# Graph attention whose row term becomes the bias of ScalarE's copies, with a later division, in a four-block transformer on one core

## Chip, core and metric

One core of one Trainium2 chip runs the whole computation in one launch. The metric is the device time in microseconds (us); three runs of the kernel before gave 1117.23, 1118.01 and 1122.63, so its median is 1118.01. Engines are named as the profile does: PE (TensorE matmuls), PEld (TensorE weight loads), DVE (VectorE), ACT (ScalarE), POOL (GpSimd), SP (SyncE, which issues DMAs). Each engine runs its own instructions strictly in order and waits on semaphores.

## What is computed

The input is `x` (4 graphs of 256 rows of 256) and a context (4 x 256 x 64). Four blocks follow one another: a two-layer graph attention, a mixture of 8 experts (top 2), a learned mix with a sparse similarity, and a transformer layer with 32 heads and 32 experts (top 8). The change touches only the first block:

```python
x = x + gat(ctx, adj=_layernorm(x))           # two layers of:
feat = einsum('nf,hfo->hno', x, W)            # 8 heads of 32
attn_self  = einsum('hno,ho->hn', feat, a_self)
attn_neigh = einsum('hno,ho->hn', feat, a_neigh)
e = attn_self[:, :, None] + attn_neigh[:, None, :]     # 256 x 256 a head
e = leaky_relu(e, 0.2) + MASK_VAL * (1.0 - adj)
alpha = softmax(e, axis=-1)
out = elu(einsum('hnm,hmo->hno', alpha, feat) + b)
```

Everything is in float32; the edge term and some projections go through PE as `float32r`, a rounded form of it.

## The kernel before, in words

**Rounds, units, quads.** The graph attention handles (layer, graph) pairs in `ROUNDS` = 8 rounds, layer 0 for the four graphs and then layer 1. A round has `UNITS` = 8 units, one for each head; a unit is a 256 x 256 matrix of edges, held as two tiles of 128 rows side by side (128 x 512). Four units form a quad. The 64 units run through a software pipeline that every engine writes out as a loop over slots k; in slot k an engine treats unit k less its own lag, in the order of the code. `starts_in(k, lead)` names the round that starts `lead` slots later, `quad_at(k, lag)` the quad due `lag` slots after its base, `round_at(k, lag)` the same for a round of layer 1. The loop ends at `LAST` = 75.

**The stations of unit k.** (1) PE `edges` writes the logits into one of two PSUM banks `ZB` (L606): the neighbour term, the same for all rows, by a matmul whose stationary operand is -1 in the row of head h and whose moving operand is `st_parts`, 256 columns read twice; then the row term by two matmuls of 256 columns with `st_parts` as stationary operand and a constant as moving operand. (2) ACT `copy_z` (L1025) copies the bank into `alpha`, a ring of six, in one 128 x 512 copy, times 0.2 in odd units. (3) The leaky part: DVE `leak` in even units, two POOL instructions in odd ones. (4) DVE `edges` adds the mask and takes the row minimum. (5) ACT `exps` takes the exponential of each tile with the row sum. (6) PE `turn` transposes four 128 x 128 blocks into `PTB`. (7) ACT or DVE copies them to `alphaT` (`copy_T`; DVE in odd units, but for every sixteenth).

**The stations of quad j.** DVE `invert` takes reciprocals of the row sums in slot 4j+7. PE `weigh` in slot 4j+9 multiplies by the features into `OB`, and spreads the reciprocals by 16 small matmuls. DVE `divide` (slot 4j+10) multiplies the two; POOL `positive` and ACT `exp_out` (also 4j+10) form the two halves of the elu, DVE `elu` (4j+11) joins them into `h1T`, the input of layer 1, or `x1T`, which PE turns (`turn_x1`, 17 slots after the round's start), DVE adds to `xs` (`add_x1`, 18) and measures (19), and POOL takes the inverse deviation of (20).

**Before a round.** Four slots before it starts, PE `prep` computes the self and neighbour terms of all heads into `MISC`, and DVE `prep` splits them into a high and a low part, `st_parts`. PE `features` computes one tile of features three slots ahead and the other two slots ahead, and ACT `copy_features` takes them out one slot ahead; its start is where I cut the rounds below. In layer 0 `prep` and `features` contract over 64 values in one matmul, in layer 1 over 256 in two.

**What sets the order.** Nothing but the slots and these waits: PE's `edges(k)` needs `copy_z(k-2)` finished, since there are two `ZB` banks; `turn(k)` needs `exps(k)`; `weigh(j)` needs `divide(j-2)`. SP loads all expert weights (24 loads of 512 KB) during the first 48 us, behind the small loads, one of which is the indicator array `ind_f` of 48 x 8 x 144 values, which ACT rounds to float32r once (L1072).

## Time and profile before

| What | Value |
|---|---|
| median of three runs | 1118.01 us |
| the profiled execution itself | 1124.08 us, with a span of 1122.3 us from its first to its last instruction |
| mean granted TensorE clock | 0.947 of 2.4 GHz |
| PE / PEld / DVE / ACT / POOL busy over the span | 93% / 75% / 76% / 54% / 38% |
| graph attention, first feature copy to last edge copy | 12.4 to 182.8 us |
| DVE's transposed copies (L1590, 128 x 512) | 28, mean 685 ns |
| ACT's edge copies (L1029, 128 x 512) | 64, mean 593 ns |
| ACT's exponentials (L1042, 128 x 256) | 128, mean 505 ns, with a sum read of 196 ns each |
| POOL's two instructions of an odd unit (L1386, L1389) | 32 each, mean 2035 and 1314 ns |
| DVE's 128 x 256 copy out of PSUM (L1601) | 16, mean 422 ns |

A matmul's busy time overlaps that of its neighbours, and so does an activation's, so what one of them costs on a full engine is the distance from its start to the next start. A profile execution is one sample; this one lies 0.5% above the median of the runs. The clock column of a table of stretches gives the granted share of the full 2.4 GHz: 0.50 is 1.2 GHz. Before 55 us it has no record and prints 1.00.

### The profile page before, as it was taken

The numbers are of one execution on the slowest core, as the hardware profiler recorded it, in microseconds if no ns is written. First come the engines' busy times: TensorE is split into PE (matmuls) and PEld (weight loads), VectorE is DVE, ScalarE is ACT, GpSimd is POOL, SyncE is SP. The second block draws the span as 40 slices with busy tenths as digits, with TensorE's granted clock in tenths as the row PEclk, the third lists the DMA queues.
The fourth block names the chain that finished last, engine by engine and source line by source line (L and its number), as shares of the span: only waits on it lengthen the run. The fifth ranks groups of instructions, "written<-read, shape, count | busy, mean of one in ns | idle before, by whom it ended". The sixth has DMA issues, their size and how long they took to land.

```text
span 1122.3 us, 20301 instructions
## 1 busy us (share of the span) xinstructions
PE 1041.2 (93%) x6046; PEld 845.9 (75%) x6046; DVE 857.1 (76%) x2625; ACT 605.4 (54%) x1686; POOL 422.8 (38%) x365
## 2 busy tenths in 40 slices
PE   5888988899999369999999999999998999999997
PEld 3555665456666247899999999999987888888886
DVE  6878687567773689877777777776878878878877
ACT  3578686533333167777777778777953222222221
POOL 5679696251110543332423334222323323323221
PEclk9979697599999589999999999999999999999999
DMA  9600000311111420110001010000010111111111
GB/s 298 242 1 1 1 2 20 104 38 48 45 43 32 125 67 6 44 37 3 17 32 39 2 34 2 1 2 1 16 30 15 44 55 42 50 48 42 53 45 37
DMA packets 50259, 49.46 MB, mean 44 GB/s; under 512 B 4976, under 2 KB 43440, under 8 KB 50176
## 3 DMA queue, kind: packets, MB, share of 16 engines
q1 hardware_dynamic: 47024, 41.96, 11.8%
q0 software_dynamic: 1872, 5.11, 1.7%
q10 hardware_dynamic: 1280, 1.38, 0.5%
q8 instruction: 41, 0.67, 0.2%
q14 instruction: 42, 0.34, 0.1%
HBM read 43.32 MB, written 5.11 MB: 43 GB/s over the span
## 4 chain that ended last, share of the span: by engine, by line
PE 76%; DVE 10%; ACT 6%; POOL 4%; issue 3%; DMA 1%; SPq 0%; ACTq 0%; DVEq 0%; POOLq 0%
PE bank L58 13%; PE bank L59 12%; PE bank L60 12%; PE bank L936 6%; PE bank L957 4%; PE bank L831 4%; PE bank L839 4%; PE bank L858 4%; PE bank L946 3%; PE bank L958 2%; PE bank L629 2%; PE bank L645 2%; PE bank L615 1%; POOL rest L1386 1%; ACT alpha L1042 1%
## 5 line engine op out<-in xcount | busy, mean ns | idle before, releaser
L1451 POOL TENSOR_TENSOR rot_s<-swap,rq 128x512 f32<-128x512 f32 x64 | 88.6, 1385 | 194.4 <-ACT swap L1233 194.3
L1109 ACT ACTIVATE silu<-bank 128x512 f32<-128x512 f32 x66 | 39.6, 600 | 173.4 <-PE bank L60 173.4
L1246 ACT ACTIVATE prob<-prob,pmin 128x128 f32<-128x128 f32 (+1 forms) x256 | 113.8, 449 | 5.5 <-DVE pmin L1992 5.5
L2011 DVE TENSOR_TENSOR o_ring<-bank,o_ring 128x256 fp32r<-128x256 f32 x128 | 54.3, 424 | 80.1 <-ACT o_ring L1262 78.6
L936 PE MATMUL bank<-kv,norm 128*128 128x128 f32 (+1 forms) x512 | 106.1, 330 | 6.4 <-DVE norm L1985 6.0
L1834 DVE SCALAR_TENSOR_TENSOR xs<-bank,wt,xs 128x256 f32<-128x256 f32 x264 | 109.1, 477 | 0.1
L1407 POOL TENSOR_TENSOR gate_r<-gate_w,gate_r 128x256 fp32r<-128x256 f32 x31 | 36.5, 1176 | 177.2 <-ACT gate_r L1102 177.2
L1262 ACT ACTIVATE o_ring<-bank 128x256 fp32r<-128x256 f32 x128 | 48.5, 379 | 75.8 <-PE bank L958 75.7
L58 PE MATMUL bank<-wo_r,o_ring 128*128 128x256 f32 x256 | 82.4, 322 | 0.0
L2004 DVE TENSOR_SCALAR prob<-prob,pinv 128x128 f32<-128x128 f32 (+1 forms) x256 | 77.1, 344 | 4.6
L1992 DVE CUSTOM_DVE_ANT_0 prob<-bank,causal 128x128 f32<-128x128 f32 (+1 forms) x256 | 80.4, 352 | 0.1
L957 PE MATMUL bank<-probT,kv 128*128 128x256 f32 x256 | 76.9, 382 | 3.3 <-DVE o_ring L2011 3.3
L1812 DVE TENSOR_TENSOR hidf<-silu,bank 128x512 f32<-128x512 f32 x66 | 45.4, 688 | 44.8 <-ACT silu L1109 43.2
L58 PE MATMUL bank<-actT_r,wqk_r 128*128 128x512 f32 x144 | 71.8, 499 | 2.5 <-DVE kv L1958 2.5
L936 PEld LDWEIGHTS bank<-kv,norm 128*128 128x128 f32 x512 | 67.6, 192 | 7.4 <-DVE norm L1985 6.7
L58 PE MATMUL bank<-down_r,hidT 128*128 128x256 f32 x248 | 70.2, 283 | 2.7 <-DVE xs L1834 1.4
L60 PE MATMUL bank<-wo_r,o_ring 128*128 128x256 f32 x256 | 72.2, 282 | 0.0
L59 PE MATMUL bank<-wo_r,o_ring 128*128 128x256 f32 x256 | 72.0, 281 | 0.0
L1386 POOL TENSOR_SCALAR rest<-alpha 128x512 f32<-128x512 f32 x32 | 65.1, 2035 | 13.6 <-ACT alpha L1029 11.1
L60 PE MATMUL bank<-down_r,hidT 128*128 128x256 f32 x248 | 70.2, 283 | 0.0
L59 PE MATMUL bank<-down_r,hidT 128*128 128x256 f32 x248 | 70.1, 283 | 0.0
L1256 ACT ACTIVATE probT<-bank 128x384 f32<-128x384 f32 x128 | 62.9, 492 | 13.4 <-PE bank L946 7.9
(297 smaller groups left out, 3126.4 us busy)
## 6 DMA issues: line engine op xcount, KB each, us to landing
gate_w<-in_Wg SPq DMA_DIRECT2D x33, 128.0 KB, 2.2
up_w<-in_Wu SPq DMA_DIRECT2D x33, 128.0 KB, 2.2
down_w<-in_Wd SPq DMA_DIRECT2D x33, 128.0 KB, 2.2
w_all<-in_w_gate SPq DMA_DIRECT2D x8, 512.0 KB, 10.7
w_all<-in_w_up SPq DMA_DIRECT2D x8, 512.0 KB, 10.3
w_all<-in_w_down SPq DMA_DIRECT2D x8, 512.0 KB, 10.6
wq_g<-in_Wq SPq DMA_DIRECT2D x4, 1024.0 KB, 5.5
wo_g<-in_Wo SPq DMA_DIRECT2D x4, 1024.0 KB, 5.3
```

The costliest lines, as they stand in the source:

```text
L58: pe.matmul(out, lhs[0], rhs[0], start=first, stop=False)
L59: pe.matmul(out, lhs[0], rhs[1], start=False, stop=False)
L60: return pe.matmul(out, lhs[1], rhs[0], start=False, stop=last)
L936: mm = pe.matmul(S_BANK[u % 2][:, nt * P:nt * P + (nt + 1) * P], qT[:, (u // 2) % 4, b2 * N + nt * P:b2 * N + nt * P + P], kT[:, b * N:b * ...
L957: pe.matmul(O_BANK[:, 0:N], vt[:, t, :], probT[:, u % 2, 0:N], start=True, stop=False)
L1246: ins = act.activation(prob[:, u % 4, nt * P:nt * P + (nt + 1) * P], prob[:, u % 4, nt * P:nt * P + (nt + 1) * P], ACT.Exp, bias=pmin[:, u ...
L1256: act.activation(probT[:, u % 2, :], PT_BANK[:, 0:3 * P], ACT.Copy).then_inc(S["pT_copied"], 1)
L1386: pool.tensor_scalar(rest[:], alpha[:, k % RING, :], 1.0 / NEG - 1.0, 0.0, ALU.mult, ALU.min).then_inc(S["z_rest"], 1)
L1451: pool.tensor_tensor(rot_s[:, m % 2].rearrange("p (b n) -> p b n", b=2), swap[:, m % 2].rearrange("p (b n) -> p b n", b=2), bcast(tab[:, 1 ...
L1834: ins = dve.scalar_tensor_tensor(xs[:, t, :], DB[2 * (mod % 2) + j // 2][:, j % 2 * D:j % 2 * D + D], w, xs[:, t, :], ALU.mult, ALU.add)
L1992: ins = dve.tensor_tensor_reduce(out=prob[:, u % 4, nt * P:nt * P + (nt + 1) * P], in0=S_BANK[u % 2][:, nt * P:nt * P + (nt + 1) * P], in1 ...
L2004: ins = dve.tensor_scalar(prob[:, u % 4, nt * P:nt * P + (nt + 1) * P], prob[:, u % 4, nt * P:nt * P + (nt + 1) * P], pinv[:, u % 4, nt:nt ...
```

## The change

The row term leaves the 128 x 512 edge matrix. The indicator array shrinks to two values a head (`ind[:, h, 0]` for the neighbour term, `ind[:, :, 1]` for all heads' row terms). A new PE step `self_columns(r)`, three slots before a round, computes the row term of all eight heads as columns (two matmuls of 8 columns) into `MISC`; a new DVE step `keep_columns(r)` in the same slot copies them into `s_col`, times 0.2 for odd heads. `edges(k)` on PE is a single matmul of 256 columns, and `copy_z(k)` on ACT makes two copies of 128 x 256 from it, one a tile, each with its column of `s_col` as bias.

Besides that: ACT hands every sixteenth unit's transposed copy to DVE; `divide` moves one slot later, `positive`, `exp_out` and `elu` two; the steps behind a round of layer 1 (`turn_x1`, `add_x1`, the measure and the inverse) move two slots later, and with them the ends of the three normalisations and `LAST`; DVE's `neighbours(0)` moves ahead of `measure(1)`. A spare array keeps the other arrays nearly where they were. The whole diff:

```diff
--- before.py
+++ after.py
@@ -31,7 +31,6 @@
 QUAD = 4
-PAD = 16
 RING = 6
...
@@ -179,7 +178,7 @@
         qkT = first_use.enter_context(nc.sbuf_tensor("qkT", [FC, 2, B * N], F32))
-        ind_f = first_use.enter_context(nc.sbuf_tensor("ind_f", [TR, GH, P + PAD], F32))
+        ind_f = first_use.enter_context(nc.sbuf_tensor("ind_f", [TR, GH, 2], F32))
         first_use.close()
...
@@ -188,10 +187,13 @@
         wst1 = sb_early("wst1", [P, HC, TR])
-        ind = sb_early("ind", [TR, GH, P + PAD], F32R)
+        ind = sb_early("ind", [TR, GH, 2], F32R)
         st_parts = sb_early("st_parts", [TR, 2, N], F32R)
...
         neg_rstd = sb_early("neg_rstd", [P, T])
+        sb_early("spare", [P, 1120])
+        s_col = sb_early("s_col", [P, 2, NT, GH])
+        s_scale = sb_early("s_scale", [P, NT, GH // 2, 2])
         row_sum = sb_early("row_sum", [P, 2, NT, QUAD])
...
@@ -313,7 +315,7 @@
-            "st_ready", "feat_ready", "feat_copied", "st_copied", "adj_ready",
+            "st_ready", "col_ready", "col_copied", "feat_ready", "feat_copied", "st_copied", "adj_ready",
             "adj_bias", "z_ready", "z_copied", "z_rest", "z_pool", "z_dve", "edge_done", "alpha_done", "alphaT_ready",
...
@@ -342,8 +344,8 @@
         ALLQ = ROUNDS * QUADS
-        LAST = ALL + 11
-        NORM_AT, TURN_AT, ROUTE_AT = (ALL, ALL + 2, ALL + 8), (ALL + 2, ALL + 4, ALL + 9), (ALL + 4, ALL + 6, ALL + 10)
+        LAST = ALL + 13
+        NORM_AT, TURN_AT, ROUTE_AT = (ALL, ALL + 2, ALL + 10), (ALL + 2, ALL + 4, ALL + 11), (ALL + 4, ALL + 6, ALL + 12)
...
@@ -366,7 +368,7 @@
         def copied_by_dve(k):
-            return k % 2 == 1 and k % 16 != 15
+            return k % 2 == 1
...
@@ -591,6 +593,18 @@
+                def self_columns(r):
+
+                    if r == 0:
+                        pe.wait_ge(S["ind_done"], 1)
+                    else:
+                        pe.wait_ge(S["col_copied"], r)
+                    pe.wait_ge(S["st_copied"], 2 * r + 2)
+                    for nt in range(NT):
+                        mm = pe.matmul(MISC[:, N + nt * GH:N + nt * GH + GH], st_parts[:, r % 2, nt * P:nt * P + P],
+                                       ind[:, :, 1], start=True, stop=True)
+                    mm.then_inc(S["col_ready"], 1)
+
                 def features(r, nt):
...
@@ -606,19 +620,11 @@
                     r, h = divmod(k, UNITS)
-                    if k == 0:
-                        pe.wait_ge(S["ind_done"], 1)
-                    if h == 0:
-                        pe.wait_ge(S["st_copied"], 2 * r + 2)
                     if k >= 2:
                         pe.wait_ge(S["z_copied"], k - 1)
-                    pe.matmul(ZB[k % 2].rearrange("p (u n) -> p u n", u=NT), ind[:, h, 0:P],
-                              bcast(st_parts[:, r % 2, :], 1, NT), start=True, stop=False)
-                    for nt in range(NT):
-                        mm = pe.matmul(ZB[k % 2][:, nt * N:nt * N + N].rearrange("p (u n) -> p u n", n=PAD),
-                                       st_parts[:, r % 2, nt * P:nt * P + P],
-                                       bcast(ind[:, h, P:], 1, N // PAD), start=False, stop=nt == NT - 1)
-                    mm.then_inc(S["z_ready"], 1)
+                    pe.matmul(ZB[k % 2][:, 0:N], ind[:, h, 0:1].to_broadcast([TR, P]), st_parts[:, r % 2, :],
+                              start=True, stop=True
+                              ).then_inc(S["z_ready"], 1)
...
@@ -692,6 +698,7 @@
                     features(0, nt)
+                self_columns(0)
                 for k in range(-1, LAST):
...
@@ -699,12 +706,14 @@
                         edges(k + 1)
+                    if (r := starts_in(k, 3)) is not None:
+                        self_columns(r)
                     for nt in range(NT):
...
                         weigh(j)
-                    if (r := round_at(k, 17)) is not None:
+                    if (r := round_at(k, 19)) is not None:
                         turn_x1(r)
...
@@ -1026,7 +1035,13 @@
                         act.wait_ge(S["alphaT_ready"], k - RING + 1)
-                    act.activation(alpha[:, k % RING, :], ZB[k % 2][:], ACT.Copy, scale=NEG if k % 2 else 1.0).then_inc(S["z_copied"], 1)
+                    r, h = divmod(k, UNITS)
+                    if h == 0:
+                        act.wait_ge(S["col_copied"], r + 1)
+                    for nt in range(NT):
+                        ins = act.activation(alpha[:, k % RING, nt * N:nt * N + N], ZB[k % 2][:, 0:N], ACT.Identity,
+                                             bias=s_col[:, r % 2, nt, h:h + 1], scale=NEG if k % 2 else 1.0)
+                    ins.then_inc(S["z_copied"], 1)
...
@@ -1078,7 +1093,7 @@
                         copy_T(k - 5)
-                    if (j := quad_at(k, 1)) is not None:
+                    if (j := quad_at(k, 3)) is not None:
                         exp_out(j)
...
@@ -1377,7 +1392,7 @@
             for k in range(LAST):
-                if (j := quad_at(k, 1)) is not None:
+                if (j := quad_at(k, 3)) is not None:
                     positive(j)
...
@@ -1392,7 +1407,7 @@
                     inverse(k // 2)
-                if (r := round_at(k, 20)) is not None:
+                if (r := round_at(k, 22)) is not None:
                     inverse(r)
...
@@ -1507,6 +1522,8 @@
+                dve.memset(s_scale[:, :, :, 1:2], NEG)
+                dve.memset(s_scale[:, :, :, 0:1], 1.0)
                 chain.link(dve.memset(wst0[:], 0.0))
...
@@ -1565,6 +1582,14 @@
+                def keep_columns(r):
+
+                    dve.wait_ge(S["col_ready"], r + 1)
+                    if r >= 2:
+                        dve.wait_ge(S["z_copied"], UNITS * (r - 1))
+                    dve.tensor_tensor(s_col[:, r % 2].rearrange("p u h -> p (u h)"), MISC[:, N:N + NT * GH],
+                                      s_scale[:].rearrange("p u a j -> p (u a j)"), ALU.mult).then_inc(S["col_copied"], 1)
+
                 def leak(k):
...
@@ -1628,8 +1653,9 @@
                 prep(0)
+                keep_columns(0)
+                neighbours(0)
                 measure(1)
-                neighbours(0)
                 for k in range(LAST):
...
@@ -1647,15 +1673,17 @@
                         prep(r)
+                    if (r := starts_in(k, 3)) is not None:
+                        keep_columns(r)
                     if (j := quad_at(k, -2)) is not None:
                         invert(j)
-                    if (j := quad_at(k, 1)) is not None:
+                    if (j := quad_at(k, 2)) is not None:
                         divide(j)
-                    if (j := quad_at(k, 2)) is not None:
+                    if (j := quad_at(k, 4)) is not None:
                         elu(j)
-                    if (r := round_at(k, 18)) is not None:
+                    if (r := round_at(k, 20)) is not None:
                         add_x1(r)
-                    if (r := round_at(k, 19)) is not None:
+                    if (r := round_at(k, 21)) is not None:
                         measure(r)
...
@@ -2101,10 +2129,10 @@
-    ind = np.zeros((TR, GH, P + PAD), np.float32)
+    ind = np.zeros((TR, GH, 2), np.float32)
     for h in range(GH):
-        ind[[h, ROW + h], h, :P] = -1.0
-        ind[[GH + h, ROW + GH + h], h, P:] = -1.0
+        ind[[h, ROW + h], h, 0] = -1.0
+        ind[[GH + h, ROW + GH + h], h, 1] = -1.0
...
```

## Rows read from the trace of the kernel before

**Rows 1.** Stretches, one a round: length; PE, PEld, DVE, ACT, POOL busy; clock; DMA share, GB/s.

```profile
...
12.36:32.96 20.60, 14.69 (x45) 9.97 (x45) 18.41 (x52) 11.15 (x32) 17.47 (x16) 1.00 1.06 369
32.96:58.61 25.65, 24.99 (x132) 15.57 (x130) 20.73 (x61) 15.94 (x48) 15.43 (x11) 1.00 0.56 194
58.61:81.25 22.64, 20.47 (x126) 12.96 (x126) 18.08 (x56) 15.99 (x50) 17.50 (x12) 0.70 0.00 1
81.25:99.00 17.75, 16.09 (x132) 10.83 (x132) 15.48 (x48) 15.29 (x49) 15.96 (x11) 1.00 0.01 2
99.00:117.33 18.33, 16.00 (x132) 10.82 (x132) 15.67 (x50) 15.66 (x50) 16.43 (x11) 1.00 0.00 1
117.33:143.09 25.76, 25.03 (x133) 15.78 (x132) 16.42 (x52) 15.81 (x49) 16.60 (x11) 0.60 0.00 1
143.09:161.94 18.85, 16.68 (x138) 11.27 (x136) 17.31 (x54) 15.81 (x49) 16.99 (x13) 1.00 0.00 1
161.94:182.18 20.24, 18.45 (x118) 12.14 (x119) 14.89 (x52) 13.76 (x42) 15.75 (x12) 0.66 0.01 2
...
```

**Rows 2.** Timeline of PE in round 5: start us, busy us, instructions.

```profile
...
127.14 0.79 PE L615 MATMUL bank<-st_parts,ind 48*128 48x512 f32 x1
127.74 0.63 PE L618 MATMUL bank<-ind,st_parts 48*128 48x256 f32 x2
128.29 1.94 PE L590 MATMUL bank<-actT,wst 128*48 128x256 f32 x4
...
134.56 2.07 PE L602 MATMUL bank<-w,actT 128*128 128x256 f32 x4
136.56 1.94 PE L645 MATMUL bank<-alphaT,rq 128*32 128x256 f32 x16
...
139.28 1.12 PE L629 MATMUL bank<-ident,alpha 128*128 128x128 f32 x4
140.32 0.52 PE L615 MATMUL bank<-st_parts,ind 48*128 48x512 f32 x1
...
```

**Rows 3.** Timeline of PE in round 1.

```profile
...
46.27 1.08 PE L590 MATMUL bank<-ctx_all,wst 64*48 64x256 f32 x2
47.28 1.11 PE L629 MATMUL bank<-ident,alpha 128*128 128x128 f32 x4
...
```

**Rows 4.** Timeline of PE in round 3.

```profile
...
86.63 0.50 PE L615 MATMUL bank<-st_parts,ind 48*128 48x512 f32 x1
86.97 0.40 PE L618 MATMUL bank<-ind,st_parts 48*128 48x256 f32 x2
87.30 0.66 PE L629 MATMUL bank<-ident,alpha 128*128 128x128 f32 x4
...
```

**Rows 5.** Timeline of ACT in round 3.

```profile
...
85.13 0.61 ACT L1029 ACTIVATE alpha<-bank 128x512 f32<-128x512 f32 x1
85.61 0.53 ACT L1042 ACTIVATE alpha<-alpha,edge_min 128x256 f32<-128x256 f32 x1
...
86.10 0.53 ACT L1042 ACTIVATE alpha<-alpha,edge_min 128x256 f32<-128x256 f32 x1
...
87.47 0.51 ACT L1060 ACTIVATE g_exp<-g_out,bT 128x256 f32<-128x256 f32 x1 [0.75 <-DVE g_out L1602]
87.89 0.58 ACT L1029 ACTIVATE alpha<-bank 128x512 f32<-128x512 f32 x1
...
```

**Rows 6.** Timeline of ACT: four copies of 128 columns out of PSUM.

```profile
...
381.17 1.15 ACT L1195 ACTIVATE actT<-bank,lnw 128x128 f32<-128x128 f32 x4 [1.04 <-PE bank L896]
...
```

**Rows 7.** Groups by line and form, 0 to 330 us: busy us, mean ns, idle before.

```profile
...
L1314 ACT ACTIVATE sim<-bank 128x256 f32<-128x256 f32 x8 | 3.0, 380 | 0.4 <-PE bank L557 0.3
...
```

**Rows 8.** Waits from 12 to 190 us: who for whom, total, times, longest.

```profile
...
ACT g_exp L1060 <- DVE g_out L1602: 29.6, 15, 4.1
...
POOL g_pos L1364 <- DVE g_out L1602: 22.4, 15, 3.9
DVE g_pos L1601 <- PE bank L650: 15.2, 8, 5.2
...
```

## The prediction

> **What bounds the kernel now.** The edit lives in the graph attention, eight rounds of eight units (a unit is one head of one graph). I read the stretch table first, cut where ScalarE starts the copy of each round's features [rows 1]. The reader is to see two kinds of round. Rounds 3, 4 and 6 (17.75, 18.33, 18.85 us) have the TensorE clock at its full level, 2.4 GHz, and no engine full: PE 16.0 to 16.7, POOL 16.0 to 17.0, DVE 15.5 to 17.3, ACT 15.3 to 15.8 busy. Rounds 1 and 5 (25.65, 25.76) have PE busy for 25.0 of it and everybody else below 21: there PE is the bound, because it runs at 1.2 GHz. Round 5 shows it as a mean clock of 0.60. Round 1 is printed as 1.00, but its four transposes take 1.11 us [rows 3], the same as at 139.28 in round 5 while the clock is down (1.12) [rows 2], so it was slow too. Rounds 2 and 7 are mixed. Round 0 (20.60) has PE idle for 6 us and DVE busy for 18.4: no PE edit moves it.
>
> Next the PE order of a slow round, start to start [rows 2]: transposes of a unit 139.28 to 140.32, 1.04; its edge term, one 512-column and two 256-column matmuls, 127.14 to 128.29, so 1.15; `prep` 1.9; `features` 2.0 a tile; `weigh` 136.56 to 139.28, so 2.7. In layer 0 `prep` takes 46.27 to 47.28, 1.0 [rows 3]; a tile of `features` has the same contraction and the same 256 columns there, and I give it 1.0 too. A layer-0 round at 1.2 GHz is 8 x (1.04 + 1.15) + 2 x 2.7 + 1.0 + 2.0 = 25.9 us; round 1 has 25.65, so the sum is the explanation of that round. With layer-1 `prep` and `features` it is 28.8; round 5 is shorter because its first 2.6 us and its last part are fast. Last the table of waits [rows 8]: in-order engines lose 29.6 us (ACT) and 22.4 (POOL) on `g_out`, that is on `divide`, which itself waits 15.2 for PE's `weigh`.
>
> **The change, part by part.**
> Edge matmuls: 64 units go from three matmuls (1024 columns) to one of 256. The new one costs a half of the pair of 256-column ones: 0.28 of 1.15 at 1.2 GHz [rows 2]; at 2.4 GHz 0.17 of 0.67 [rows 4]. Saved: 0.87 or 0.50 us of PE a unit, 7.0 or 4.0 a round. On the path only where PE is the bound. `self_columns` adds two matmuls of 8 columns a round; no row has the form, between 0.05 and 0.56 (the price of the 256-column pair); I take 0.2. A slow PE round is then 25.9 - 7.0 + 0.2 = 19.1 in layer 0, 28.8 - 6.8 = 22.0 with layer-1 `features`.
>
> ScalarE's copies: one immediate-scale copy of 512 columns, 0.48 start to start [rows 5], becomes two of 256 with a bias column. The two ends: the exponential of `exp_out`, same size, bias column, from SBUF, 0.42 start to start [rows 5]; and the four 128-column copies out of PSUM with a scale column in 1.15 us [rows 6]: 0.37 of it for the last, so 0.26 each. 256 more columns cost a copy out of PSUM about 0.60 - 0.38 = 0.22 us (512 columns in [rows 5] against 256 in [rows 7]), 128 more 0.11, so 0.37. A pair is 0.74 to 0.84, and a unit grows by 0.26 to 0.36; I take 0.30, nearer the PSUM row. A round: ACT slots now 8 x (0.48 + 2 x 0.49) + 4.5 x 0.48 (transposed copies, the same form) + 2 x 0.42 + 0.48 = 15.2; plus 2.4, less half a transposed copy (0.24) = 17.3. So ACT takes POOL's place as the busiest, and its 2 to 3 us of spare time per fast round is spent. This is the price of the edit.
>
> The Trainium skill ("ScalarE: Activation LUTs", What ACT_TABLE_LOAD costs) gives an ACTIVATE 186 ns + 0.833 ns an element and adds 93 ns for each column operand, with 93 ns of overlap back to back. By it, an estimate, the pair costs 2 x 0.40 against 0.52, +0.28 a unit, inside my ends; the trace's fixed part of a 512-column copy agrees (0.60 us busy, 0.48 apart).
>
> DVE: 4 transposed copies come over from ACT (0.69 us each, one in two rounds), `keep_columns` adds a 128x16 product a round (below the 0.42 us of 128x256 rows, above nothing: 0.15). About 0.5 us a round on an engine with over 2 us spare in fast rounds. Its place matters more. It sits in the slot of `features`, and waits for `self_columns`, which on PE stands behind that slot's transposes and edge matmul; `elu` and the next edges queue behind it, and ACT's exponentials for them. And PE waits in `self_columns` for DVE's `prep` one slot after it was issued, where before it waited three slots later; `features` and `weigh` queue behind. From 0 to about 1 us a round (half a slot of 2.2); seven rounds; I take 1.5 in all, 0 and 7 as ends.
>
> The later `divide`, `positive`, `exp_out`, `elu`: no work is added. The waits of [rows 8] have one or two slots more of cover; a wait that is not the bound gives nothing by itself, but ACT, now fullest, needs those 2.5 us a round. I count this as what lets rounds be near ACT's sum, not as a term. `turn_x1`, `add_x1` and `measure` go with it; the next user of those banks is `features` of round 7, one slot behind `add_x1` of round 4, so it still fits. The two further slots at the end contain no instruction of their own. Tail: 0 (-0.5 to +1).
>
> Start: the indicator load shrinks from 221 KB to 3 KB and ACT's copy of it with it, but PE was waiting for the weights then; `neighbours(0)` moves ahead of a `measure`; `self_columns` and `keep_columns` stand ahead of the first copy. Together -0.1 (-1 to +0.5), in round 0.
>
> **The sum.** A fast round today is some 1.2 us above its fullest engine (18.3 against 16.0 to 17.0 in rounds 3, 4, 6 [rows 1]). Above ACT's 17.3 that gives 18.5. A slow one cannot be under 19.1 or 22.0. The clock: PE now has 65% or so of its fast work left, so I expect it at 1.2 GHz for most of the stage, with full speed after the dense stretches (`features` and `weigh` stand together, and in round 5 the clock rises right behind them: the 512-column matmul at 140.32 takes 0.52 where the one at 127.14 took 0.79 [rows 2]). If a fifth of the time is fast, PE's 22.0 becomes 22.0 / 1.2 = 18.3, no longer above ACT. I take 19.0 to 19.4 in layer 0 and 19.5 with layer-1 features. New minus old by round: 0: -0.1; 1: 19.4 - 25.65 = -6.3; 2: 19.0 - 22.64 = -3.6; 3: 19.5 - 17.75 = +1.8; 4: +1.2; 5: -6.3; 6: +0.6; 7 (no features): 18.8 - 20.24 = -1.4. Sum -14.1; with the new waits +1.5: **-12.6**. The profiled execution took 1124.08 (span 1122.3), so 1111.5 for such a one; the median of the runs is 6 us under it, and 1118.0 - 12.6 = **1105.5**.
>
> What follows the stage starts earlier and is not shortened. Where the clock changes after it may shift by some us either way: 2 us in the range.
>
> **Rivals.**
> A, ACT alone is the bound: the clock or PE's shorter queue keeps PE out of it, and the later division removes all of ACT's waits. Seven rounds of 17.8: 20.5 + 124.6 = 145.1 against 169.8 now (rounds 0 to 7), -24.7: 1093. For: 29.6 us of ACT's waits. Against: fast rounds today never reach their fullest engine.
>
> B, the low clock eats the gain: today's three fast rounds (54.9 us) become slow ones of 21 to 22 while rounds 1, 2, 5 get to 20 to 21. (20.5 + 2 x 20 + 4 x 21.5 + 20) = 166.5: -3.3, 1115. For: rounds 3, 4, 6 keep the full clock with PE 88% busy, and the stage has dropped to 1.2 GHz in rounds 2, 5 and 7 with lighter stretches. The Trainium skill ("TensorE: Matmul & The Clock Gate", Part 1) states the same direction, activity releases the throttle, and its Part 4 that transposes do not count as busy the same way. By that rule the edge matmuls removed are what kept the clock up, and B or C would be the outcome; the trace agrees that a PE full of transposes and edge terms stays at 1.2 GHz from 127.1 to 136.6 us [rows 2].
>
> C, slower: at 1.2 GHz the heavy slots stop overlapping. `prep` 3.2, `features` + `weigh` 6.2, `features` 3.3, `weigh` 4.1 are PE's, and in the other four slots PE must wait for ACT (17.3 / 8 = 2.16 each), since only two edge banks let it run ahead: 16.8 + 8.6 = 25.4 for rounds 3 to 6, 22.5 for 1 and 2, 21 for 7: 20.5 + 45 + 101.6 + 21 = 188.1, +18.3: 1136 in full, 1126 if half of it comes. It is slower from a mean of 21.3 us over rounds 1 to 7. Against: PE ran 25.0 of 25.7 us in round 1, so slots do overlap.
>
> **Chances.** Forecast 0.55; A 0.20; B 0.15; C 0.10. Range 1096 to 1116: all of the forecast's own spread (ACT's ends give 2 us either way on seven rounds, waits -1.5 to +5.5, the clock's share 5), half of A, and B. The least that a measurement tells from no change is 0.5%, 5.6 us. Faster by more: forecast, A and a part of B, 0.79; within 0.5%: most of B, 0.12; slower: 0.09.
>
> **What would show it.** Edge matmul 0.28 apart at 1.2 GHz and PE busy under 20 us a round; two ACT copies 0.37 to 0.42 apart and ACT busy 17 to 18 a round; rounds 1, 2 and 5 near 19.5 and rounds 3, 4, 6 about 1 us longer than now; a mean clock under 0.75 over the stage; the wait of `g_exp` below 10 us in total; ACT as the largest name in the chain between 30 and 180 us. It is wrong if rounds 3, 4 and 6 grow past 21.3, if a new wait on the column product is above 1 us a round, or if a transfer or table load shows up in the stage.

## The result, and the profile after

The changed kernel takes 1115.06 us (median of 14 runs, 1114.27 to 1118.13); the kernel before, on the same chips, 1121.32 (14 runs, 1117.23 to 1126.49). The ratio is 0.9949, 95% interval 0.9933 to 0.9964: faster by 5.7 us, less than half of the 12.6 that were forecast. The median lies just inside the forecast's range of 1096 to 1116, and near rival B's 1115. A part of the distance from 1105.5 to 1115.06, 3.3 us, is the base: the three first runs gave 1118.01, the larger sample 1121.32. The profiled execution took 1115.82 (span 1114.0), 8.3 us under that of before, which lay 2.8 above its median. So the rounds below explain 8 us, of which the medians hold 6.

Stretches of the changed kernel, one a round as in [rows 1], last the stretch from the last pair of edge copies to just past the end of the stage:

```profile
...
11.79:31.02 19.23, 11.60 (x33) 6.67 (x33) 18.15 (x55) 13.00 (x39) 16.50 (x15) 1.00 1.04 364
31.02:53.76 22.74, 18.52 (x115) 10.72 (x113) 19.97 (x64) 16.98 (x56) 15.22 (x11) 0.85 0.71 247
53.76:74.38 20.62, 17.70 (x112) 10.40 (x112) 17.28 (x57) 17.05 (x56) 16.30 (x12) 0.67 0.00 2
74.38:92.92 18.54, 16.10 (x118) 10.11 (x118) 14.04 (x45) 17.06 (x56) 15.55 (x11) 0.82 0.01 1
92.92:112.86 19.94, 15.83 (x118) 9.97 (x118) 16.22 (x53) 17.18 (x57) 15.85 (x11) 0.83 0.01 2
112.86:132.87 20.01, 16.05 (x118) 10.09 (x118) 16.24 (x52) 17.16 (x56) 15.84 (x11) 0.83 0.00 1
132.87:152.97 20.10, 16.83 (x122) 10.60 (x122) 17.99 (x57) 17.24 (x56) 16.23 (x13) 0.83 0.01 2
152.97:173.00 20.03, 15.45 (x104) 9.17 (x104) 17.26 (x50) 15.08 (x49) 16.24 (x12) 0.67 0.00 1
173.00:194.50 21.50, 16.66 (x132) 12.50 (x132) 15.50 (x50) 9.97 (x28) 8.63 (x10) 0.66 0.19 58
...
```

The stage is 8.45 us shorter: its first feature copy comes 0.57 earlier, rounds 0 to 7 take 161.21 against 169.82, and the tail 20.9 against 20.2. From ScalarE's last copy of the stage (193.94, before 202.39) to the end both have 920 us. The reader is to see that rounds 4 to 7 now all take 19.9 to 20.1, and that no engine is full in any of them: ACT has 17.2 (15.1 in round 7), PE 15.5 to 16.8, DVE 16.2 to 18.0. PE's clock stands at 0.82 or 0.83 in rounds 3 to 6, where it was 1.00 in three of them. With two levels, 0.50 and 1.00, a mean of 0.82 is full speed for about two thirds of a round.

Who waited for whom in the changed kernel, 12 to 190 us (total, times, longest), against [rows 8]:

```profile
...
POOL rest L1401 <- ACT alpha L1042: 27.8, 14, 3.8
...
ACT alpha L1042 <- PE bank L625: 24.2, 18, 2.5
...
DVE alpha L1604 <- POOL alpha L1404: 19.4, 19, 1.9
PE bank L635 <- DVE alphaT L1615: 13.6, 7, 3.0
...
POOL g_pos L1379 <- DVE g_out L1627: 3.5, 2, 2.8
...
ACT g_exp L1075 <- DVE g_out L1627: 1.7, 1, 1.7
...
```

The waits for `g_out` are gone (29.6 to 1.7 for ACT; 22.4 to 3.5 for POOL). Others have taken their place: POOL for ACT's copies 27.8 us (11.1 before), ACT for the edge matmul 24.2 (12.4), DVE for POOL 19.4 (11.8), PE for DVE's transposed copies 13.6 (3.4). One round shows how they hang together. PE in round 5:

```profile
...
116.21 1.09 PE L635 MATMUL bank<-ident,alpha 128*128 128x128 f32 x4 [2.17 <-DVE alphaT L1615]
117.23 0.58 PE L625 MATMUL bank<-st_parts,ind 48*128 48x256 f32 x1
117.73 1.93 PE L651 MATMUL bank<-alphaT,rq 128*32 128x256 f32 x16
119.44 1.08 PE L656 MATMUL bank<-ident,row_sum 128*32 128x128 f32 x16
120.45 1.12 PE L635 MATMUL bank<-ident,alpha 128*128 128x128 f32 x4
121.50 0.58 PE L625 MATMUL bank<-st_parts,ind 48*128 48x256 f32 x1
...
122.72 0.38 PE L625 MATMUL bank<-st_parts,ind 48*128 48x256 f32 x1
123.03 1.06 PE L592 MATMUL bank<-actT,wst 128*48 128x256 f32 x4
...
128.24 1.07 PE L651 MATMUL bank<-alphaT,rq 128*32 128x256 f32 x16
129.13 0.62 PE L656 MATMUL bank<-ident,row_sum 128*32 128x128 f32 x16
129.68 0.66 PE L635 MATMUL bank<-ident,alpha 128*128 128x128 f32 x4
...
```

DVE (L1604 is the mask step, L1615 the transposed copy), POOL (L1401 and L1404 are its two instructions of an odd unit) and ACT (L1042 is the pair of edge copies) in the same round, one timeline each:

```profile
...
113.64 0.41 DVE L1604 CUSTOM_DVE_ANT_0 alpha<-alpha,norm 128x256 f32<-128x256 f32 x1
...
113.97 1.48 DVE L1604 CUSTOM_DVE_ANT_0 alpha<-alpha,norm 128x256 f32<-128x256 f32 x1
...
115.39 0.68 DVE L1615 COPY alphaT<-bank 128x512 f32<-128x512 f32 x1
...
```

```profile
...
113.70 1.47 POOL L1404 TENSOR_TENSOR alpha<-alpha,rest 128x512 f32<-128x512 f32 x1
...
118.62 1.30 POOL L1404 TENSOR_TENSOR alpha<-alpha,rest 128x512 f32<-128x512 f32 x1
123.04 1.92 POOL L1401 TENSOR_SCALAR rest<-alpha 128x512 f32<-128x512 f32 x1 [3.13 <-ACT alpha L1042]
...
```

```profile
...
117.84 0.84 ACT L1042 ACTIVATE alpha<-bank,s_col 128x256 f32<-128x256 f32 x2
118.57 0.51 ACT L1057 ACTIVATE alpha<-alpha,edge_min 128x256 f32<-128x256 f32 x1
...
122.11 0.84 ACT L1042 ACTIVATE alpha<-bank,s_col 128x256 f32<-128x256 f32 x2 [2.46 <-PE bank L625]
...
130.68 0.84 ACT L1042 ACTIVATE alpha<-bank,s_col 128x256 f32<-128x256 f32 x2 [0.28 <-PE bank L625]
...
```

Read it as one chain. A mask step on DVE at 113.97 takes 1.48 us beside POOL's sum at 113.70, instead of the 0.41 of the one before it; behind it in DVE's order stands the transposed copy (115.39), which frees a transpose bank; PE, idle for 2.17 us, turns the next unit at 116.21, and only then `weigh` at 117.73; the edge matmul stands behind `weigh` and the next transposes, at 121.50; ACT, idle for 2.46, copies it at 122.11; POOL, which has ended at 119.92, starts again at 123.04, after 3.13 us of idle. The Trainium skill ("SBUF — State Buffer", Who interferes with whom) says that a DVE instruction with two SBUF inputs contends with a GpSimd instruction that reads SBUF, and that the one issued second fully blocks. The trace fits it: of the mask steps of this kernel, seven that started while POOL's sum (L1404) ran took 1.48 or 1.49 us and one 1.23, while twelve that had started before the sum took 0.39 to 0.42. No run here takes one of the two instructions away.

The clock has a part in this chain. The round has two `weigh`s. The one at 117.73 runs at 1.2 GHz (granted clock 0.50 from 116 to 122 us) and takes 2.72 us to the next transposes (120.45); ACT then stands idle for 2.46 us. The one at 128.24 runs at 2.4 GHz (1.00 from 123 us on) and takes 1.44 us (to 129.68); ACT's idle behind it is 0.28. The second `weigh` of round 1 has the same place and ran at 1.2 GHz. PE and ACT there:

```profile
...
47.83 1.93 PE L651 MATMUL bank<-alphaT,rq 128*32 128x256 f32 x16
49.53 1.08 PE L656 MATMUL bank<-ident,row_sum 128*32 128x128 f32 x16
50.55 0.68 PE L635 MATMUL bank<-ident,alpha 128*128 128x128 f32 x4
...
```

```profile
...
51.57 0.84 ACT L1042 ACTIVATE alpha<-bank,s_col 128x256 f32<-128x256 f32 x2 [2.35 <-PE bank L625]
...
```

It takes 2.72 us and ACT idles 2.35. Over the rounds, the second `weigh` is slow in rounds 1, 2 and 7, with 2.35, 2.31 and 1.70 us of ACT's idle behind it, and fast in rounds 3 to 6, with 0.28 or 0.29. The first `weigh` is slow in rounds 1 to 7, with 1.20 to 2.46. So what ACT waits for is the order, edge matmul behind `weigh`, at a low clock. At the full clock the order costs next to nothing, and experiment 4 takes the order away and leaves the clock.

ACT's pair of copies is 117.84 to 118.57 = 0.73 us, so a unit costs ACT 0.25 more (0.30 taken). PE's edge matmul, ahead of `weigh`, is 117.23 to 117.73 = 0.50 us at 1.2 GHz where I had 0.28, and 122.72 to 123.03 = 0.31 at the full clock for 0.17 [rows 4]. Half a pair was the wrong row for a matmul that stands alone.

### The profile page after: what moved, and what is told of

Its sections match the earlier page's. It is cut to its first block, busy times and chain, and to the rows that moved or that the text cites. A ratio compares the mean times of both kernels' runs of the same rounds, so it can differ in the third digit from the quotient of the medians.

```text
span 1114.0 us, 20158 instructions
## 1 busy us (share of the span) xinstructions
PE 1020.6 (92%) x5934; PEld 827.6 (74%) x5934; DVE 858.1 (77%) x2639; ACT 614.0 (55%) x1746; POOL 418.8 (38%) x365
## 4 chain that ended last, share of the span: by engine, by line
PE 75%; DVE 10%; ACT 5%; POOL 4%; issue 4%; DMA 1%; SPq 0%; ACTq 0%; DVEq 0%; POOLq 0%
PE bank L57 13%; PE bank L58 13%; PE bank L59 13%; PE bank L945 6%; PE bank L966 5%; PE bank L840 4%; PE bank L848 4%; PE bank L867 4%; PE bank L955 3%; PE bank L967 2%; PE bank L635 2%; PE bank L651 2%; DVE alpha L1604 2%; POOL ytok L1496 1%; POOL rest L1401 1%
## 5 line engine op out<-in xcount | busy, mean ns | idle before, releaser
L635 PE MATMUL bank<-ident,alpha 128*128 128x128 f32 x256 | 54.3, 350 | 31.9 <-DVE alphaT L1615 13.6
L1604 DVE CUSTOM_DVE_ANT_0 alpha<-alpha,norm 128x256 f32<-128x256 f32 x128 | 61.5, 517 | 19.6 <-POOL alpha L1404 19.4
L1401 POOL TENSOR_SCALAR rest<-alpha 128x512 f32<-128x512 f32 x32 | 63.9, 1996 | 29.3 <-ACT alpha L1042 27.8
L635 PEld LDWEIGHTS bank<-ident,alpha 128*128 128x128 f32 x256 | 35.9, 176 | 49.9 <-ACT alpha L1057 27.0
L57 PE MATMUL bank<-down_r,hidT 128*128 128x256 f32 x248 | 70.3, 283 | 2.7 <-DVE xs L1862 1.4
```

What stands on the lines that cost most here:

```text
L57: pe.matmul(out, lhs[0], rhs[0], start=first, stop=False)
L635: mm = pe.transpose(PTB[k % 2][:, mc * N + nt * P:mc * N + nt * P + P], alpha[:, k % RING, nt * N + mc * P:nt * N + mc * P + P], ident[:])
L1604: ins = dve.tensor_tensor_reduce(out=alpha[:, k % RING, nt * N:nt * N + N], in0=alpha[:, k % RING, nt * N:nt * N + N], in1=adj[:, r % B, n ...
```

## The experiments

Each was timed together with the kernel before on one chip, 4 to 12 executions of it; ratios are to that kernel, with their 95% intervals. The changed kernel is 0.9949 (0.9933 to 0.9964) on that scale.

**1 and 2. The two parts alone.** `later_only`: the kernel before with the later slots of the change; the steps behind a round and `LAST` move too.

```diff
...
-                    if (j := quad_at(k, 1)) is not None:
+                    if (j := quad_at(k, 3)) is not None:
                         exp_out(j)
...
-                if (j := quad_at(k, 1)) is not None:
+                if (j := quad_at(k, 3)) is not None:
                     positive(j)
...
-                    if (j := quad_at(k, 1)) is not None:
+                    if (j := quad_at(k, 2)) is not None:
                         divide(j)
-                    if (j := quad_at(k, 2)) is not None:
+                    if (j := quad_at(k, 4)) is not None:
                         elu(j)
...
```

> The kernel before with nothing but the later steps (divide one slot, positive, exp_out and elu two, the steps behind a round two, two slots more at the end). Theory P (in the rounds at 1.2 GHz PE is full, so only PE's own work counts): rounds 1 and 5 stay at 25 to 26 us, the rounds at 2.4 GHz lose up to 1 us each, -1 to -3 us in all; the wait of g_exp drops from 29.6 to under 10 us all the same. Rival L (the gain of the change comes from the later division, the shorter PE work does little): -5 us or more.

Measured 0.9971 (0.9945 to 0.9996), -3.3 us by the ratio, with 0.4 and 6.2 as its ends. `g_exp` waits 2.1 us (29.6), and ACT waits 36.2 us for the edge matmul instead (12.4 before). Round 1 stays at 25.3 as theory P has it, but round 5 does not: it takes 20.67, with a mean clock of 0.92 against 0.60, while round 3 grows from 17.75 to 20.22 at 0.79. One execution doesn't say whether the order or the clock gave the gain.

`row_only`: the changed kernel with those slots put back.

> The changed kernel with the division and all that follows it at the old slots: the row term as bias alone. Theory P with ACT as the fullest engine: ACT's 17.3 us a round plus some 2.5 us of waits for g_out, rounds of 20 to 22 us, between -4 and +6 us against the kernel before. Rival L: the row term alone gives nothing or loses, +3 us or more. Rival M (the two parts are independent and add): the changed kernel's -6 less what the later division gave alone.

Measured 0.9997 (0.9978 to 1.0016): nothing. ACT waits 25.7 us for `g_out`, rounds 1 to 6 take 19.3 to 23.4. Alone the row term shows no gain. Rival M expected the changed kernel's -6 less the other part, about -3; the parts' gains add to 0.32% against 0.51% for both, and with these intervals that is not a difference, so this run doesn't decide whether the parts simply add. Experiment 11 shows it for `pair_z`.

**3. ScalarE's price.** `one_copy`:

```diff
...
-                    for nt in range(NT):
-                        ins = act.activation(alpha[:, k % RING, nt * N:nt * N + N], ZB[k % 2][:, 0:N], ACT.Identity,
-                                             bias=s_col[:, r % 2, nt, h:h + 1], scale=NEG if k % 2 else 1.0)
+                    ins = act.activation(alpha[:, k % RING, :].rearrange("p (u n) -> p u n", u=NT),
+                                         bcast(ZB[k % 2][:, 0:N], 1, NT), ACT.Copy, scale=NEG if k % 2 else 1.0)
...
```

> The changed kernel, but ScalarE makes one copy of 128 x 512 that reads the 256 columns twice, with no bias: the row term is left out of the result, and the columns are still computed. ACT's cost of a unit falls from two copies (0.84 us for the pair in the trace of the changed kernel, 0.73 start to start to the next) to one of about 0.48. Theory R (a round of the changed kernel is set by the chain PE edge matmul, ACT copy, POOL, DVE, ACT exponentials, PE transposes, in which the copy is one link, and by PE's in-order weigh): 0.25 us a unit, 16 us in the stage, of which a half or less shows: -4 to -8 us against the changed kernel. Rival A (ACT is the bound): all of it, -13 us or more. Rival N (the copy is hidden): less than 2 us.

Measured 0.9927 (0.9902 to 0.9952), 2.5 us better than the changed kernel. The two intervals overlap; taken together they leave anything from about -6 to +1 us (an estimate). That excludes rival A's -13 and doesn't part theory R from rival N. Of the 16 us of ACT work a third at most is on the path: ScalarE alone is not the bound.

**4. The edge matmul ahead of `weigh`.** `pair_z`: two units share a bank, and both are written in the odd slots.

```diff
...
+        def z_half(k):
+            return bank[2 + k // 2 % 2][:, k % 2 * N:k % 2 * N + N]
...
-                    if 0 <= k + 1 < ALL:
+                    if k % 2 and k + 1 < ALL:
                         edges(k + 1)
+                        edges(k + 2)
...
```

> The changed kernel with the edge matmuls of two units written one behind the other into one bank, in the odd slots, ahead of weigh: units k+1 and k+2 in slot k. So both edge terms are there before PE starts weigh, and ACT has a unit more in hand. Theory R (ACT waits 24.2 us for the edge matmul that stands behind weigh on PE, POOL 27.8 us behind it): these waits fall below 10 us, rounds 1 to 7 go from 20.3 to 18.5 to 19.5 us, -6 to -12 us against the changed kernel. Rival B (the clock or PE's own work is what sets a round): the waits move to the transposes, within 2 us of the changed kernel. Rival C (ACT cannot start before both matmuls are done): 1 to 4 us slower.

Measured 0.9917 (0.989 to 0.9944), 3.6 us better than the changed kernel by the ratios, under the 6 to 12 of theory R. The two intervals overlap a little, so the trace has to carry it:

```profile
...
PE bank L639 <- DVE alphaT L1620: 30.0, 15, 3.3
...
POOL rest L1406 <- ACT alpha L1047: 11.8, 14, 2.1
...
ACT alpha L1047 <- PE bank L628: 7.4, 15, 1.0
...
```

ACT's wait on the edge matmul is 7.4 us (24.2), POOL's on ACT 11.8 (27.8). Rounds 3 to 6 take 18.6 to 19.3, as theory R had it, and rounds 1 and 2 take 21.2 and 20.0. ACT's idle for the edge matmul behind a `weigh` is under 0.7 us, at either clock: with the edge matmuls in front, a slow burst no longer holds ACT. What has grown is PE's wait for DVE's transposed copies: 30.0 us from 13.6. The edit did a second thing that I hadn't expected: side by side the matmuls are cheaper again. PE of `pair_z`:

```profile
...
66.60 1.09 PE L639 MATMUL bank<-ident,alpha 128*128 128x128 f32 x4 [2.08 <-DVE alphaT L1620]
67.62 0.79 PE L628 MATMUL bank<-st_parts,ind 48*128 48x256 f32 x2
68.21 0.42 PE L607 MATMUL bank<-ind,st_parts 48*128 48x8 f32 x2
...
```

67.62 to 68.21 is 0.59 for two at 1.2 GHz, ahead of the small matmuls of `self_columns`. In the same place a single one takes 0.38 in the changed kernel (46.04 to 46.42), so the second adds 0.21. Ahead of `weigh` two take 0.73 (116.20 to 116.93 in this trace) against 0.50 for one. So of the 3.6 us a part may be PE's work and not its order; this run doesn't part them.

**5 and 6. The clock.** `filled` adds three more edge matmuls a unit into the unused half of the bank. `pair_fill` adds three to `pair_z`, into the unit's own half, ahead of the one that counts.

```diff
...
+                    for extra in range(3):
+                        pe.matmul(ZB[k % 2][:, N:2 * N], ind[:, h, 0:1].to_broadcast([TR, P]), st_parts[:, r % 2, :],
+                                  start=True, stop=True)
...
```

> The changed kernel with three more edge matmuls of 256 columns a unit on PE, written into the unused half of the same bank and read by nobody: PE streams 1024 columns a unit for the edge term again, as the kernel before, and ScalarE's part stays changed. Theory K (the low clock of the changed kernel comes from the columns that are gone, and costs time): the mean clock of rounds 3 to 6 goes from 0.82 to 0.95 or more, and where PE is fast a round stays at 18.5 to 19.5; slow rounds return to 24 to 26 us. Whole: -2 to +6 us against the changed kernel. Rival W (a round is set by PE's work whatever the clock): rounds of 21 to 25 throughout, +8 to +15 us. Rival R (the clock does not matter since PE waits anyway): within 2 us.

Measured 1.0025 (0.9998 to 1.0052), +8.5 us on the changed kernel by the ratios: more than theory K's +6 and inside rival W's +8 to +15. The clock went up only in part: rounds 3 to 6 have 1.00, 0.84, 0.85, 0.91. Round 3 of this kernel:

```profile
...
83.93:103.26 19.33, 16.19 (x142) 11.45 (x142) 15.99 (x47) 17.06 (x57) 15.95 (x11) 1.00 0.01 2
...
```

At the full clock throughout, it takes 19.33, while round 3 of the changed kernel takes 18.54 at 0.82. Rounds 4 to 7 take 20.78, 22.53, 19.46 and 18.77, and the largest cost of the fillers is in rounds 1 and 2 (27.45, 24.65), where PE has 26.8 and 23.4 us busy. This doesn't show that the low clock is free: the fillers stand ahead of every edge matmul, and ACT's waits for that matmul grow from 24.2 to 37.6 us. It shows that the clock can't be bought back this way.

> The paired edge matmuls (pair_z) with three more matmuls of 256 columns a unit. Theory K: pair_z has the slack to take them at 2.4 GHz, the clock of rounds 3 to 6 goes from 0.82 to 0.91 up to 0.95 or more, and the time is within 3 us of pair_z either way. Rival W: +6 us or more, since the fillers stand ahead of weigh and the transposes.

Measured 0.9973 (0.9954 to 0.9991), +6 us on `pair_z`; the clock is 0.75 to 0.83 in rounds 3 to 6, below the 0.82 to 0.91 of `pair_z`, with 1024 columns of edge matmuls a unit on PE again. Rival W, and theory K's rise of the clock didn't come. So the number of these columns alone doesn't set the clock.

**7 and 8. A shorter burst.** `split_weigh` and `pair_split` issue the 16 spreading matmuls of `weigh` one slot later.

```diff
...
                     if (j := quad_at(k, 0)) is not None:
                         weigh(j)
+                    if (j := quad_at(k, 1)) is not None:
+                        spread_sums(j)
...
```

> The changed kernel, with the second half of weigh (the 16 small matmuls that spread the reciprocals, 1.0 us at 1.2 GHz, 0.55 at 2.4) one slot later, so that a unit's transposes and its edge matmul stand between the halves. No work is added or removed. Theory R (the in-order burst of PE ahead of the next edge matmul is what stalls ACT and POOL): two bursts a round get 0.55 to 1.0 us shorter, up to 1.5 us a round, -3 to -9 us. Rival D (divide and what follows come later by as much and give it back, or the clock falls because the dense stretch is gone): -1 to +4 us.

Measured 0.9939 (0.9918 to 0.9961): the changed kernel's time, inside rival D's range. Theory R's -3 to -9 us didn't come, though ACT's wait for the edge matmul fell from 24.2 to 17.7 us: DVE's wait for the spreading matmuls rose to 7.9 and PE's for DVE's transposed copies from 13.6 to 18.8. Rounds in the profile scatter from 18.1 to 23.9, the longest at a mean clock of 0.71.

> pair_z and split_weigh together. Theory R: pair_z has already taken the edge matmul out from behind weigh, so the split has little left to give: -2 to +1 us against pair_z. Rival T (in pair_z the transposes behind weigh are the next wait, 19 us of PE weight loads on the exponentials and ACT on DVE's minima): another -3 us or more, since the transposes come between the halves.

Measured 0.9964 (0.9947 to 0.9982), 5 us worse than `pair_z`. A new wait of ACT's exponentials on the spreading matmuls (21.1 us) came with it: in the code, the exponentials of a quad wait until the spreading matmuls of the quad two before it have read its row sums. Theory R's "-2 to +1 us" fails here for something that I hadn't priced: who else waits for the moved step.

**9. ScalarE's price in `pair_z`.** `pair_one` is `pair_z` with the single copy of experiment 3.

> pair_z with ScalarE's one copy of 512 columns and no bias (the row term is left out of the result). Theory A2 (with the edge matmul out from behind weigh, ScalarE is the bound: no idle of it for 15 us on end in rounds 3 and 4 of pair_z): the 0.25 us a unit now shows in full where it did to 2.5 us of 16 in the changed kernel, -8 to -14 us against pair_z, rounds of 16.5 to 17.5. Rival T (POOL and DVE, at 16.8 us a round, take over at once): -2 to -5 us.

Measured 0.9868 (0.9837 to 0.9899), 5.5 us better than `pair_z` by the ratios, 3.0 by the medians. The ratio lies between the two cases, the medians in rival T's. The intervals overlap, so its size is open (an estimate of 1 to 10 us), but it is not the 14 us of a full bound.

**10. DVE's order.** `copy_first` is the changed kernel with one step moved:

```diff
...
+                    if 0 <= k - 5 < ALL and copied_by_dve(k - 5):
+                        copy_T(k - 5)
                     if 0 <= k - 2 < ALL:
                         edges(k - 2)
                     if 0 <= k - 1 < ALL and (k - 1) % 2 == 0:
                         leak(k - 1)
-                    if 0 <= k - 5 < ALL and copied_by_dve(k - 5):
-                        copy_T(k - 5)
...
```

> The changed kernel, with DVE's transposed copy ahead of the edge steps in a slot instead of behind them. Theory D (PE waits 13.6 us for DVE's transposed copies, because they stand in order behind the steps that wait for POOL): that wait falls below 5 us, and PE reaches weigh and the next edge matmul sooner, -2 to -5 us. Rival E (DVE then waits for PE's transposes with the mask step behind it, and ACT's exponentials behind that): 0 to +6 us, with a new wait of DVE on PE's transposes.

Measured 0.9891 (0.9864 to 0.9918), 6.5 us better than the changed kernel and 12.2 better than the kernel before. PE's wait on these copies:

```profile
...
PE bank L635 <- DVE alphaT L1615: 3.7, 3, 1.5
...
DVE alphaT L1615 <- PE bank L635: 1.7, 1, 1.7
...
```

3.7 us, from 13.6; DVE's new wait on PE is 1.7. Theory D, by more than it asked. The clock of this execution is higher in two rounds, 0.91 in round 5 and 1.00 in round 7 against 0.83 and 0.67, so a part of the gain may come by way of the clock; no run parts the two.

**11. The division in `pair_z`.** `pair_early` puts the slots of before into `pair_z`.

> pair_z with divide, positive, exp_out and elu at the old slots. Theory R: what the later division gives is the same hiding of weigh from ACT, POOL and DVE as before, and without it g_exp waits 20 us or more again: +4 to +8 us against pair_z. Rival I (the pair ahead of weigh makes the later division idle): within 2 us of pair_z.

Measured 0.9995 (0.9976 to 1.0014), 8.7 us worse than `pair_z`; `g_exp` waits 27.9 us again. Alone (experiment 1) the later slots gave 0.29%, here they give 0.78%. In `pair_z` the later division is a condition of what the shorter PE work gives; rival I is out.

**12. Both orders.** `pair_first` is `pair_z` with experiment 10's move.

> pair_z with DVE's transposed copy first, where PE waits 30.0 us for it. Theory D: -2 to -5 us against pair_z. Rival E: 0 to +6 us. Rival S (PE has slack there, so its wait costs nothing, and ACT is the bound): within 2 us.

Measured 0.9828 (0.9801 to 0.9855), median 1102.16: 19 us faster than the kernel before, 13 to 14 than the changed one, and 10 than `pair_z`, twice what theory D asked. PE's wait for DVE's copies is 6.3 us, from 30.0. Rivals E and S are out. Its rounds:

```profile
...
11.72:31.85 20.13, 11.62 (x35) 6.96 (x35) 19.05 (x55) 12.84 (x40) 17.31 (x16) 1.00 1.04 367
31.85:51.58 19.73, 16.48 (x112) 10.19 (x112) 19.49 (x60) 16.78 (x56) 14.89 (x11) 0.91 0.75 261
51.58:70.63 19.05, 15.90 (x112) 9.98 (x112) 18.85 (x55) 16.96 (x57) 16.44 (x12) 0.73 0.01 2
70.63:88.52 17.89, 15.46 (x120) 10.16 (x118) 15.84 (x50) 17.05 (x56) 15.18 (x10) 0.81 0.01 1
88.52:107.02 18.50, 12.74 (x118) 8.44 (x118) 17.18 (x54) 17.05 (x56) 17.21 (x12) 1.00 0.01 2
107.02:125.38 18.36, 14.95 (x115) 9.42 (x116) 16.31 (x52) 16.94 (x56) 15.74 (x11) 0.81 0.00 1
125.38:143.98 18.60, 13.98 (x127) 9.18 (x125) 16.36 (x55) 17.07 (x57) 15.62 (x12) 1.00 0.01 2
143.98:158.99 15.01, 10.56 (x102) 6.98 (x102) 13.79 (x42) 14.75 (x50) 14.36 (x10) 0.89 0.01 2
...
```

Rounds 1 to 6 are 17.9 to 19.7. Rounds 4 and 6 have the full clock and take 18.50 and 18.60, rounds 3 and 5 have 0.81 and take 17.89 and 18.36. In this kernel, where nothing short stands behind `weigh`, the lower clock shows no cost. In `pair_first_act_b`, whose time is the same, rounds 3 and 4 (1.00 and 0.91) take 17.98 and round 5 (0.82) 19.02, so it isn't shown to be free.

**13. Was it there before?** `before_first_b` is the kernel before with the move of experiment 10.

> The kernel before with DVE's transposed copy ahead of its edge steps. Theory X (the hold of PE by DVE's copy order is a bound that the change exposed: PE waits only 3.4 us for DVE's transposed copies in the trace of before, and is full at 1.2 GHz anyway): within 2 us of the kernel before. Rival Y (the order costs the same in both kernels, so it does not belong to the change): -5 us or more.

Measured 1.0021 (0.9998 to 1.0044): nothing gained, and rival Y is out. The place of DVE's copies costs time only since the change.

**14 and 15. What is left.** In `pair_first_act_b` ScalarE's transposed copy stands ahead of its exponentials too.

> pair_first with ScalarE's transposed copy, too, ahead of its exponentials. Theory D carried on (whoever holds a transpose bank holds PE): -1 to -3 us against pair_first. Rival E (PE now waits for the exponentials, 19.5 us and 40.3 us of weight loads, and these come later by a copy in every other slot, while ACT waits for the transposes with them behind it): +1 to +6 us.

Measured 0.9832 (0.9806 to 0.9858), the time of `pair_first`: neither case.

> pair_first with one ScalarE copy of 512 columns and no bias (the row term is left out of the result): the price of the second copy where PE's two waits are gone. Theory A2 (now ScalarE is the bound): 0.25 us a unit, -8 to -14 us against pair_first. Rival T (POOL and DVE at 16 to 17 us a round are as full): -2 to -5 us, as in pair_one.

Measured 0.9806 (0.9784 to 0.9829), 2.5 us under `pair_first`. The intervals overlap (an estimate of -6 to +1 us), so even this cost isn't clear of noise; theory A2's -8 to -14 is out. What bounds `pair_first` is no one engine: in its rounds 4 and 5 ACT, DVE and POOL have 15.7 to 17.2 each. In the chain that ended last between 10 and 170 us, DVE's three largest lines have 32%, POOL's two 17%, ACT's two 10% and PE's three 8%; in the changed kernel, between 10 and 195 us, PE's four largest had 35%.

## Why the prediction was wrong, and what of it held

| Round | before | forecast | after | PE busy after |
|---|---|---|---|---|
| 0 | 20.60 | 20.5 | 19.23 | 11.6 |
| 1 | 25.65 | 19.4 | 22.74 | 18.5 |
| 2 | 22.64 | 19.0 | 20.62 | 17.7 |
| 3 | 17.75 | 19.5 | 18.54 | 16.1 |
| 4 | 18.33 | 19.5 | 19.94 | 15.8 |
| 5 | 25.76 | 19.5 | 20.01 | 16.1 |
| 6 | 18.85 | 19.5 | 20.10 | 16.8 |
| 7 | 20.24 | 18.8 | 20.03 | 15.5 |

- **The bound before, and the direction round by round, were right.** Rounds 1, 2 and 5 lost 2.9, 2.0 and 5.8 us, rounds 3, 4 and 6 grew by 0.8 to 1.6. PE had been full at 1.2 GHz in the slow rounds; it is below 19 us in all now. ScalarE is not the largest name in the chain, as the forecast had it: its two largest lines have 8.5%, PE's four 35%.
- **PE's price was too low.** "The new one costs a half of the pair", 0.28 us at 1.2 GHz, measured 0.50 (0.38 ahead of `self_columns`): 0.65 us saved a unit and not 0.87, 1.8 us a round where PE is slow throughout. The least for such a round in layer 0 is then 20.9 us, not 19.1. It isn't what held round 1, where PE was busy for 18.5 of 22.7 us. In fast stretches it is 0.31 for 0.17, and PE has room there.
- **ScalarE's price was right as work, 0.25 for 0.30, and wrong as a limit.** It was written down as what fills ScalarE, "the price of the edit"; the three pairs of runs put its effect on the time at 2.5, 5.5 and 2.5 us (experiments 3, 9 and 15), two of them not clear of noise and none near 16.
- **The step that failed most is "A fast round today is some 1.2 us above its fullest engine. Above ACT's 17.3 that gives 18.5", and the 19.0 to 19.5 built on it.** Already its 1.2 is misread: the rows give 1.7, 1.9 and 1.5 us for rounds 3, 4 and 6 (against PE's 16.1, POOL's 16.4 and DVE's 17.3). And it took this distance over from rounds in which PE had the full clock. Measured, rounds 4 to 6 stand 2.8 to 2.9 us above ACT's 17.2 and round 1 5.8 above (2.8 above its DVE, which has 20.0), with PE 3.3 to 4.2 us from full in each. What stands there is waiting in PE's order, longer where the clock is low: the edge matmul behind `weigh` and the transposes behind DVE's copies. Taking out the second alone brings 0.9891, the 12 us of the forecast; taking out both brings 19 us. I had put the first into rival C and dismissed it because PE was busy for 25.0 of 25.7 us in round 1: a full PE hides its own order, and with some 5 us of its work gone that argument no longer held.
- **The new waits of `self_columns` and `keep_columns`** were priced at 1.5 us and show as 1.4 + 1.5 us in round 0, which got 1.4 us shorter all the same, and as nothing after.
- **The later division** was called no term but a condition. The runs confirm the condition (experiments 2 and 11: no gain without it), and alone it gives 3.3 us (0.4 to 6.2), which the sum lacked; it is already in the measured total.
- **The clock** fell, as forecast, but by less: the forecast had full speed for a fifth of the time, and 0.82 to 0.83 in rounds 3 to 6 is two thirds. The sign "under 0.75 over the stage" didn't come; it is 0.77 from 30 to 180 us. Its working has a slip too: "65% or so of its fast work" is 12 of 16 us, 75%; 65% is 12 us as a share of an 18.5 us round.
- **Rivals B and C had a part of the cause.** B's time (1115) came out, but not by its rounds: it had 21.5 for rounds 3 to 6, and they took 18.5 to 20.1. C's heavy slots that stop overlapping at 1.2 GHz are what the trace shows behind a slow `weigh`: ACT idle for 1.2 to 2.5 us, against 0.3 behind a fast one. The sum had no term for it. Filling the columns back in raised the clock of round 3 to 1.00 and left that round 0.8 us longer; of rounds 3 to 7 three got longer and two (19.46 and 18.77) shorter, 2.3 us longer in all. How much of the changed kernel's time the low clock costs stays open. The Trainium skill's rule beside B ("TensorE: Matmul & The Clock Gate", Part 4), that transposes don't count as busy in the same way, agrees with the fall of the clock after the edge columns went; it doesn't explain `pair_fill`, where they came back and the clock stayed down.
- **Start and tail**: -0.6 and +0.7 for -0.1 and 0. Round 0 gained 1.4 where nothing was expected. DVE's 18.15 of 19.23 us there is still what it stands on. Without the later slots (`row_only`) it is 19.23 as well, with them alone (`later_only`) 20.35, so the gain comes with the row term's part of the change; that graph 0's mask now comes ahead of a `measure` is a likely reason that was not tried.

Open: why DVE has 20.0 us busy in round 1 (the expert weights still load through most of it), which leaves that round as far above its fullest engine as the others; and how much of the scatter of the kernel before, 9 us over 14 runs, is the clock's.

## What to carry to other kernels

When an engine that was full is relieved, read the next bound off its order, and not only off the busy time of the others: look which short instruction that others wait for stands behind its long bursts, and which buffer release it waits for itself. Put the short producer ahead of the burst, and the copy that frees a bank ahead of steps that wait for a third engine. A lower clock on an engine with slack costs time where it lengthens a burst that another engine waits behind, so look at the waits behind slow and fast bursts of the same kind. And take a wait apart from its price: the later division removed 28 us of ACT's waits and gave 3.3 us alone, but without it the row term's part, shorter PE work and longer ScalarE work, gave nothing.

## What was not expected of the hardware

A matmul of 256 columns with its own weights took 0.50 us at 1.2 GHz ahead of `weigh`, and two of them side by side took 0.73 in the same place; at 2.4 GHz one took 0.31 and two 0.43 (57.46 to 57.89 in `pair_z`). A mask step on DVE (128 x 256, usually 0.42 us) took 1.48 or 1.49 us when it started while POOL's 128 x 512 sum on the same ring was running, and 0.42 at most when it had started first. And ScalarE's 128 x 256 activation out of PSUM with a bias column needs 0.25 us more in a pair than a single copy of 512 columns, 0.71 to 0.73 against 0.48 to 0.50.
